# Second retention: a semaphore for each of the two copies of a sequence's rows, and 15 result buffers in the first experts instead of 17

## The reference, cut to what matters

```python
x = _layernorm(x + _L0_attn_ref(x, ...))     # 4 heads, decay mask, gated
x = _layernorm(x + _L0_ffn_ref(x, ...))      # top 2 of 8 experts, F = 256
x = _layernorm(x + _L1_attn_ref(x, ...))     # 8 heads, group norm, gated
x = _layernorm(x + _L1_ffn_ref(x, ...))      # top 2 of 8 experts, F = 512
```

## Time and profile before

| What | Value |
|---|---|
| Median of 3 runs | 1235.6 us (1232.59 to 1236.72) |
| Profiled execution | 1234.53 us, span 1232.7 us |
| Mean granted TensorE clock | 0.962 |
| Busy, share of the span | PE 92%, DVE 73%, ACT 60%, POOL 59% |

### The profile page before, as it was taken

One profiled execution on the slowest core, in us unless ns is written; L12 is line 12 of the kernel. 1 busy time (PEld: TensorE's weight loads), 2 busy tenths in 40 slices (PEclk: granted clock), 3 DMA queues, 4 the chain that ended last, 5 costly groups with the idle time before them and its releaser, 6 DMA issues.

```text
span 1232.7 us, 31631 instructions
## 1 busy us (share of the span) xinstructions
PE 1128.5 (92%) x10400; PEld 1003.1 (81%) x10400; DVE 904.5 (73%) x2648; ACT 742.7 (60%) x2015; POOL 728.6 (59%) x901
## 2 busy tenths in 40 slices
PE   8999999997888999979999999976899999999992
PEld 5888888885778999857776766665899999999991
DVE  4788998888667777666887887764676666667873
ACT  2345444653556777746666777653466666666884
POOL 0247777775567777472565766566644444445675
PEclk9999999999899999999999999885999999999996
DMA  8222111201224433343321211011311111214453
GB/s 239 69 62 73 46 40 54 72 30 53 62 79 134 124 109 106 112 150 95 104 86 50 66 50 44 27 49 45 100 58 55 56 57 55 59 55 124 147 183 122
DMA packets 75424, 101.77 MB, mean 83 GB/s; under 512 B 15139, under 2 KB 51491, under 8 KB 74851
## 3 DMA queue, kind: packets, MB, share of 16 engines
q1 hardware_dynamic: 49538, 59.89, 17.0%
q0 software_dynamic: 17280, 35.69, 8.7%
q10 hardware_dynamic: 8448, 4.20, 1.2%
HBM read 59.87 MB, written 43.04 MB: 83 GB/s over the span
## 4 chain that ended last, share of the span: by engine, by line
PE 56%; DVE 20%; ACT 7%; issue 6%; POOL 5%; DMA 4%; SPq 1%; ACTq 1%; DVEq 0%; POOLq 0%
PE banks L2354 16%; PE banks L2373 10%; PE banks L1444 6%; PE banks L1462 4%; DVE a_sT L1116 3%; DMA scattered<-b_r_x,b_r_idx 2%; DVE b_sT L2120 2%; PE banks L1383 2%; PE banks L1353 2%; ACT a_r_x L260 1%; PE banks L1380 1%; PE banks L356 1%; DVE a_qm L1218 1%; PE banks L2338 1%; PE banks L1399 1%
## 5 line engine op out<-in xcount | busy, mean ns | idle before, releaser
L1866 POOL DMA_INDIRECT expert_out<-e_ysb,b_e_idx x142 | 161.3, 1136 | 153.4 <-ACT e_ysb L1974 126.8
L2354 PE MATMUL banks<-b_e_x_hi,e_w_hi 128*128 128x256 f32 x568 | 167.4, 295 | 3.2 <-ACT e_sgl L1964 1.7
L897 POOL DMA_INDIRECT expert_out<-a_e_ysb,a_e_idx x142 | 140.8, 992 | 44.4 <-issue 35.6
L2354 PE MATMUL banks<-b_e_x_hi,e_w_lo 128*128 128x256 f32 x568 | 160.5, 282 | 0.0
L477 POOL DMA_INDIRECT scattered<-a_r_x,a_r_idx x128 | 127.8, 998 | 33.9 <-issue 33.9
L2373 PE MATMUL banks<-w_dn,e_h 128*128 x1136 | 138.3, 275 | 2.2 <-DVE e_h L2166 1.6
L2373 PEld LDWEIGHTS banks<-w_dn,e_h 128*128 128x128 f32 x1136 | 132.5, 192 | 2.9 <-issue 2.8
L2166 DVE TENSOR_TENSOR e_h<-banks,e_sgl 128x512 f32<-128x512 f32 x142 | 97.0, 689 | 50.3 <-PE banks L2354 47.6
L1964 ACT ACTIVATE e_sgl<-banks 128x512 f32<-128x512 f32 x142 | 85.1, 599 | 75.5 <-DVE e_h L2166 41.8
L477 POOL DMA_INDIRECT scattered<-b_r_x,b_r_idx x112 | 110.5, 986 | 31.0 <-issue 31.0
L2154 DVE TENSOR_TENSOR e_w_lo<-w_gu,e_w_hi 128x1024 fp32r<-128x1024 f32 x71 | 87.1, 1227 | 54.3 <-ACT e_w_hi L1953 54.3
(11 more groups left out here) (385 smaller groups left out, 3293.0 us busy)
## 6 DMA issues: line engine op xcount, KB each, us to landing
a_e_xg<-scattered SPq DMA_DIRECT2D x71, 130.0 KB, 2.2
b_e_xg<-scattered SPq DMA_DIRECT2D x71, 130.0 KB, 2.1
b_cy<-expert_out SPq DMA_DIRECT2D x32, 256.0 KB, 3.3
f_y<-expert_out SPq DMA_DIRECT2D x32, 256.0 KB, 3.4
a_xT<-in_x_T SPq DMA_DIRECT2D x16, 256.0 KB, 2.9
out<-f_x ACTq DMA_DIRECT2D x16, 256.0 KB, 2.7
expert_out<-a_e_ysb,a_e_idx POOLq DMA_INDIRECT x142, 2.3
expert_out<-e_ysb,b_e_idx POOLq DMA_INDIRECT x142
```

The lines of the kernel that those rows point to most:

```text
L897: nc.gpsimd.indirect_dma_start(out=expert_out, out_offset=bass.IndirectOffsetOnAxis(ap=idx[n % HELD][:, i:i + 1], axis=0), in_=ysb[n % HEL ...
L1866: nc.gpsimd.indirect_dma_start(out=expert_out, out_offset=bass.IndirectOffsetOnAxis(ap=idx[n % 4][:, i:i + 1], axis=0), in_=ysb[n % 4][:, ...
L2354: mm = nc.tensor.matmul(bank_of(c, j)[:, i * ROWS:(i + 1) * ROWS], w_[c % RING][:, g, f:f + P], x_[c % RING][:], start=(m == 0), stop=(m = ...
```

## The change

In the second layer's router there are four semaphores for landed stores instead of two, one for each copy and parity; the first layer's router keeps its two. `wait_free` can now wait for one copy alone. L303 waits for copy 0's stores, and a new wait in front of `copy_rows` waits for copy 1's. `put_places` waits for both. The waits of SP and POOL for all stores count four semaphores. HELD goes from 17 to 15, so that the number of semaphores is the same.

```diff
-        sent_sems = [[whole.enter_context(nc.semaphore(f"sent{l}{i}")) for i in range(2)] for l in range(2)]
-        HELD = 17
+        sent_sems = [[whole.enter_context(nc.semaphore(f"sent{l}{i}")) for i in range((2, 2 * TOPK)[l])] for l in range(2)]
+        HELD = 15
...
-            def wait_free(self, eng, t):
+            def wait_free(self, eng, t, k=None):
 
                 if not isinstance(t.n, int) or t.n not in self.late:
-                    wait_count(eng, self.sent[t.odd], SCATTERS * t.half)
+                    if self.keep_logits:
+                        wait_count(eng, self.sent[t.odd], SCATTERS * t.half)
+                    else:
+                        for i in range(TOPK) if k is None else (k,):
+                            wait_count(eng, self.sent[2 * i + t.odd], SCATTERS // TOPK * t.half)
...
-                        in_=self.copy_of(j // CH, t)[:, j % CH, :], in_offset=None).then_inc(self.sent[t.odd], 16)
+                        in_=self.copy_of(j // CH, t)[:, j % CH, :], in_offset=None
+                        ).then_inc(self.sent[t.odd if self.keep_logits else 2 * (j // CH) + t.odd], 16)
...
                         if n == 0:
                             sp.wait_ge(tables.there, 2)
-                            sp.wait_ge(router.sent[0], SCATTERS * ((EARLY + 1) // 2))
-                            sp.wait_ge(router.sent[1], SCATTERS * (EARLY // 2))
+                            for k in range(TOPK):
+                                sp.wait_ge(router.sent[2 * k], SCATTERS // TOPK * ((EARLY + 1) // 2))
+                                sp.wait_ge(router.sent[2 * k + 1], SCATTERS // TOPK * (EARLY // 2))
                         if n == SURE:
                             sp.wait_ge(tables.there, 4)
                             sp.wait_ge(tables.filled, 16 * E)
-                            for i in range(2):
-                                sp.wait_ge(router.sent[i], SCATTERS * SEQS // 2)
+                            for i in range(2 * TOPK):
+                                sp.wait_ge(router.sent[i], SCATTERS // TOPK * SEQS // 2)
...
-                    for i in range(2):
-                        pool.wait_ge(router.sent[i], SCATTERS * SEQS // 2)
+                    for i in range(2 * TOPK):
+                        pool.wait_ge(router.sent[i], SCATTERS // TOPK * SEQS // 2)
...
                             nc.scalar.copy(xres[:, bass.ds(d.n * CH, CH), :], router.copy_of(0, d)[:, :, 0:D]).then_inc(x3_kept, 1)
+                            router.wait_free(act, d, 1)
                             router.copy_rows(act, d, x3_there)
...
-                            router.wait_free(act, c2)
+                            router.wait_free(act, c2, 0)
                             wait_count(act, x3_kept, c2.n - 1)
                             norm.apply(act, r, router.copy_of(0, c2)[:, :, 0:D], c2, x3_there)
```

## The result

The change makes the kernel faster: 1224.49 us in the median of 6 runs (1222.12 to 1227.94), beside 1234.67 of the kernel before (1232.59 to 1236.72, 6 runs in all). The ratio is 0.9918, with a 95% interval of 0.9902 to 0.9934. The forecast was 1222.0 with a range of 1218.5 to 1229.5. The profiled execution took 1223.06 us, its span is 1221.2.

What follows compares the result with a forecast made beforehand. The prediction took the stage as bound by TensorE plus the gaps that late rows put into it. 10.12 + 3.39 + 0.26 = 13.8 us off the profiled 1234.53, put on the median's scale, gave 1222.0 us, range 1218.5 to 1229.5.

Steps and rivals of the forecast that it cites:

- The stall at L303: Second retention: ScalarE waits 24.4 us in 12 pieces before L303, for copy 1's stores that L303 does not touch.
- the undisturbed 17.52: Length of the step from 595.34, without store wait; nine steps from 612.86 to 780.66 should fall to it, saving 10.12 us.
- TensorE's gap and 0.52 more: Each of the nine steps gains TensorE's gap before its transposes plus 0.52 us, of which 0.28 is waiting at L2423.
- The rival of the 18.14 us floor: Nine steps fall only to 18.14 us, a floor set by something other than the stores: 1229.4 us, chance 0.14.
- The table step: Tenth step, 780.66 to 804.58, where VectorE computes expert tables: 23.92 us at granted clock 0.79, to lose 3.39 us.
- the larger of the two cases: Table step: clock no longer falls and 3.39 us are saved; if it still falls, 1.95 us.
- The twelfth wait: VectorE's residual at 824.14, outside the steps, stands 2.78 us for ScalarE's rows of sequence 13; only 0.26 us counts.
- The added waits: New waits on ScalarE and in POOL's put_places: 0 forecast, at most 3.6 and 4.2 us.
- The rival that the wait only moves: ScalarE stands at L464 instead of L303, so no change: 1235.6 us, chance 0.04.
- Fifteen buffers: First experts: 15 result buffers cost 0; result 55's last store lands 1.2 us before ScalarE writes result 70.
- the slower rival: Too few result buffers: POOL's late stores hold up ScalarE's last results and the second retention; 1239.4 us, chance 0.03.
- the clock gives some back: Moved TensorE gaps make a clock fall hit another step, costing up to 5 us: 1227 us, chance 0.08.

Runs made afterwards that it cites:

- e2: The kernel after, but the wait in front of L303 asks for the stores of both copies again: 1237.18 us, ratio to before 1.0004.
- e8: The kernel after with four added matmuls ahead of the w_q matmul in each of steps 8 to 16: 1232.84 us.
- e1: The kernel before with 15 result buffers in place of 17, nothing else: 1236.07 us, ratio to before 1.000.
- e3: The kernel after, but in front of L303 odd sequences wait for both copies' stores, even ones for copy 0 alone: 1236.73 us.
- e9: The kernel before with the same added matmuls as e7: 1232.3 us, before 1236.41 in the same set.
- e11: The e9 kernel with 1 to 5 more matmuls ahead of the transposes L356 in six steps, wait kept: 1228.77 us, ratio to before 0.9931.
- e6: The kernel after with 12 result buffers in place of 15, nothing else: 1231.87 us, ratio to before 0.9969.
- e4: The kernel after with useless matmuls before TensorE's waits in the last four steps of the second retention: 1219.28 us, ratio to before 0.9853.
- e5: The kernel after with 14 result buffers in place of 15, nothing else: 1226.16 us, ratio to before 0.9919.
- e10: The e7 kernel unchanged, measured once more in other runs, beside e9 on one chip: 1214.76 us, ratio to before 0.9822.
- e7: The e4 kernel with the three TensorE gaps of over 1 us left there filled with matmuls too: 1215.29 us, ratio to before 0.9833.

## Why the prediction was right, point by point

**The stall at L303 is for stores it need not wait for.** Right, and shown: e2 puts the second copy's wait back and has the old time; after's ACT row has no idle.

**Nine steps fall to the undisturbed 17.52.** Right: 9.91 us against 10.12, with a floor of 17.53 and two steps of 17.59. That the gain per step is TensorE's gap and 0.52 more held: the waits at L2423 for `b_r_xT` (2.5 us in 9 between 595 and 781) are gone too. The rival of the 18.14 us floor fell: steps with weight sums take 17.53. That the floor is TensorE's own work is shown by e8 (0.94 us a step for 0.80 us of work).

**The table step.** 3.39 forecast, 3.85 measured, and the clock was full, as the larger of the two cases had it. The split was mis-sized. By the table step of e1, which has the wait and no fall, 1.5 us (21.60 - 20.07) belong to the wait and 2.3 to the clock; e2, e3 and e9 have 21.4 to 21.8 there without a fall. The fall in the middle of the step, behind the gap at copy 0, is gone in all kernels without the wait, and e11 shows the same with the wait kept and the gap filled. But the forecast's premise, that no gap over 0.36 us is left in a step, doesn't hold for this one. After has a gap of 2.08 us at its end, which before, at half clock, had not:

```profile
792.28 0.19 PE L409 MATMUL banks<-b_r_picked,c_tri 128*128 128x32 bf16 x1 [2.08 <-DVE b_r_picked L402]
```

The clock doesn't fall at this gap in after and in e6. In e4 and e5 it falls within it, and in e8 1.1 us behind it. That it stayed full there in after's profiled execution was luck, though the step itself loses nothing by a fall so late (20.09 us in e4 and e5). The rule that the forecast cites (the Trainium skill, "TensorE: Matmul & The Clock Gate", Part 1: The HAM clock gate), that the array is throttled by default and its activity releases the throttle, agrees with these rows in direction: the falls begin at or behind gaps of TensorE.

**The twelfth wait.** 0.26 forecast. At its own place the term was read from a stretch that had just run at half clock, where TensorE's output matmuls were slow enough (0.63 us a pair against 0.39) to hide most of VectorE's 2.78 us. At full clock it is worth 2.4 us, by e11 against e10; ACT's wait itself is longer there, 4.42 us against 3.53 in before. In after it can't be seen, because the clock falls there once more: VectorE stands 3.36 us for TensorE in place of 2.78 for ACT.

**The added waits.** 0 forecast, 0 shown: no idle before L468, and all nine steps at 17.53. The bounds of 3.6 and 4.2 us were far too wide. The rival that the wait only moves fell.

**Fifteen buffers.** 0 forecast and 0 shown by e1. The 1.2 us of room was counted too tight: the 3.46 us of the slow landing run from the start of a store's issue (705.99 to 709.45), and the forecast added them to its end. From 516.80 they end at 520.26, 2.1 us ahead of 522.37. The last store of result 56 is issued at 520.65 in before, 3.85 us behind that of result 55, and 3.85 - 2.11 = 1.7 us is the wait that one buffer fewer brings (1.71). With three fewer some 6 us are lost in the median. So the mechanism of the slower rival is real, and starts just below 15 buffers.

**What the sum missed.** It was 13.8 and the spans differ by 11.5, the medians by 10.2. The steps and the stretch ahead of 595 lost 1.68 us, and this isn't the work of the change: steps 3 to 7 sum to 83.2 us in before, in e1, which has the change's buffers, and in e10, which has all of its code; in after to 84.4. What differs is where the clock fell, as far back as the first experts. TensorE's timeline has the same gap there in before:

```profile
323.36 1.15 PE L1462 MATMUL banks<-w_dn,a_e_h 128*128 x8 [1.99 <-ACT a_e_ysb L969]
```

and in after:

```profile
323.38 2.07 PE L1467 MATMUL banks<-w_dn,a_e_h 128*128 x8 [2.01 <-ACT a_e_ysb L974]
```

In before the clock stays full behind it, in after it is at half for 3.4 us. Ahead of this place after is 0.5 us earlier than before, and from 345 us on 2.0 later. POOL carries the lateness on, for it issues its stores one behind the other with 0.30 us between them, and comes to its row norm 2.06 us later, in before and in after:

```profile
547.31 1.04 POOL L297 TENSOR_TENSOR b_cn_rstd<-b_cn_ve,c_half 128x4 f32<-128x4 f32 x1
```

```profile
549.37 1.04 POOL L297 TENSOR_TENSOR b_cn_rstd<-b_cn_ve,c_half 128x4 f32<-128x4 f32 x1
```

TensorE had caught up to 0.45 us by then (its first step starts at 530.10 against 529.65), and loses it again: behind this row norm ACT stands 4.57 us in after against 2.96 in before, and TensorE 3.13 at 551.86 against 1.52.

```profile
550.52 1.28 ACT L303 ACTIVATE b_xb<-b_cr,b_cn_rstd 128x128 f32<-128x128 f32 x4 [4.57 <-POOL b_cn_rstd L297]
```

In all profiled kernels with 15 or 17 buffers the sum of steps 3 to 7 goes with the places of the falls. It is 83.2 us in the five with a fall near 524 and one near 555 (before, e1, e9, e10, e11), 84.4 in after, with one at 552 alone, 84.7 to 84.8 in the three with one more near 538 (e2, e4, e7), and 86.2 and 86.5 in the two whose falls begin at 549 (e3, e8). No kernel moved one of these falls by itself: that they are the cause is argued from the traces and not shown. Behind the table step 0.26 was to be gained and 0.62 was lost, since the clock was at half for 41 us there against 34 before; e4, e7 and e10 show that this stretch can give 4 to 7.5 us by itself. Of the rival "the clock gives some back" a part of the amount came in, the forecast's 1222.0 being 2.5 us too low, but not at its place: after has no fall in any step between 597 and 792 us.

## What to carry to other kernels

Where one semaphore counts all transfers of a buffer group, ask which of them the waiting instruction really has to follow; the price of the wait is read by cutting the steps where the bound engine starts them and comparing with a step that has no wait. A gap on TensorE costs more than its length if the clock falls behind it, and a term read next to a stretch at half clock is too small, since the slow engine covers other waits. A buffer count can be lowered until the store that is re-used ends close to the copy that re-uses it; past that point the lateness is paid.

## What the runs showed of the hardware

The clock fell to 1.2 GHz at or behind gaps of 1.04 us (e7, at 844) to 3.13 us (after, at 552) of a TensorE that was otherwise busy, and stayed full behind others of the same length; behind one and the same gap of the program, 1.99 and 2.01 us at 323, it stayed full in before and fell in after. A fall of 10.2 us within one step cost 2.3 us where VectorE was the bound, and 4.6 where TensorE was. Filling the gaps with matmuls that compute nothing took 5 to 10 us off the kernel after.

The landings of each sequence's last store alternate in before, some 2.3 to 2.5 us for even sequences and 2.9 to 3.7 for odd ones (sequence 11's took 2.3), which is the alternation of the waits. In the stretch of the long one (706.0 to 709.5) a packet of another queue stands among the store's, in that of a short one (687.8 to 690.2) it doesn't. The DMA queues of the long stretch:

```profile
q0 software_dynamic: 64, 0.13, 11.9%
q8 instruction: 1, 0.02, 2.0%
```

and of the short one:

```profile
q0 software_dynamic: 64, 0.13, 16.7%
```

In the stretches looked at the packet and the longer landing go together. No kernel was made that moves the one without the other, so that it delays the store is not shown.
